# The hand-written step lists of a six-chain graph network kernel laid anew on four engines

## The chip, the cores and the metric

The kernel runs on one core of a Trainium2 chip. The metric is the device time of one execution in microseconds. The kernel before took 2766.72 us (median of 3 runs, 2757.14 to 2768.18).

## The reference, cut to what matters

128 graphs of 128 nodes with 256 features each pass through four residual layers. All graphs share one adjacency matrix, `adj`.

```python
def reference(x, adj, ...):
    h = relu(layernorm(x)); x = x + _L0_gnn_ref(h, adj, ...)   # 4 attention heads, elu, 1 head, elu, 2-layer FFN, layernorm
    h = relu(layernorm(x)); x = x + _L1_gnn_ref(h, adj, ...)   # masked attention with 8 heads of 32, output projection
    h = relu(layernorm(x)); x = x + _L2_gnn_ref(h, adj, ...)   # deg * (h Wi + b) + adj (h Wj)
    h = relu(layernorm(x)); x = x + _L3_gnn_ref(h, adj, ...)   # one attention head; attention output beside its values
    return x
```

## The kernel before, in words

**Tiling.** Two graphs make a pair, so there are 64 pairs. A pair's `x` is a 256 KB tile. It lies in one of 8 slots of the SBUF tensor `xs` (`PAIR_SLOTS = 8`), is loaded there, updated in place by every layer, and stored from there. Pair p+8 uses the slot of pair p.

**Steps.** The work on a pair is cut into steps named by chain: A and B are the heads of the first attention layer, C the rest of layer 0, D and F the eight-head attention of layer 1, E the layers 2 and 3. A suffix .0 or .1 means one graph of the pair. PE has 52 steps for a pair, ACT 56, DVE 83, POOL 17. A step waits on the semaphores of the steps that it reads, or whose buffer it overwrites, does its few instructions and signals. Nothing else orders the engines against each other.

**Order.** Each engine runs its own written list in rounds (`rounds`, L257). An entry `F_rb:6` in round i does step F_rb for pair i-6. The list is walked from front to back in every round, and an engine never goes past a step whose wait has not ended. A larger number thus means a later round, and the place in the list the order inside a round. The rounds of two engines are counted separately: DVE's round i+1 runs about beside PE's round i.

**Load and store.** SyncE (SP) issues both. For each pair it waits for `E_left` (DVE, both graphs) and `E_right` (POOL) of pair p, issues the store (L326), waits until that has landed, and issues the load of pair p+8 (L320). The first step that reads the new tile is `A_stats.0` of pair p+8 on DVE (L810, wait in `x_there`, L801).

**Steps that the text names.**
- `E_o` (PE, L1407), the last matmuls of a pair; `E_left` (DVE, L1026) adds the result into the left half of the slot; `E_right` (POOL, L495) adds the right half.
- `F_recip` (DVE, L978), `F_rb` (DVE, L984: a copy that spreads 16 reciprocals over 512 columns), `F_rT` (PE, L1071: four transposes of that, written to `pF`), then `F_o` (L1329).
- `A_zT` (PE, L1071 into `pA`), the first PE step of a pair; `A_f` (PE, L1080 with `wa`), `A_fround` (ACT, L549), `A_frest` (DVE, L854), `A_wh_hi` and `A_wh_lo` (PE, L1080 with `wh`); `A_wh_lo.0` waits for `A_frest`.
- `F_s` (PE, L1306) and `F_maxa`, `F_maxb` (DVE, L859), `F_suma`, `F_sumb` (DVE, L971), `C_max`, `E_max` (DVE, L859), `B_hl` (DVE, L885), `C_hlow` (DVE, L847), `E_low`, `D_low`, `A_low` (DVE, L839), `E_z`, `D_z`, `A_z` (DVE, L824), `F_x2` (DVE, L998), `B_oh` (PE, L1154), `E_h` (PE, L1384), `E_zT` (PE, L1071 into `pE`), `C_low` (POOL, L465), `D_xb` (POOL, L482), `E_rstd` (POOL, L408 and L410).

In the lists before, the stretch of DVE's list from the end of a pair to the start of the next one in the same slot, and what stands behind it, is:

```python
... E_left.0:8 E_left.1:8 C_hlow:4 F_suma.1:6 F_sumb.1:6 E_low:7 A_stats.0:0 B_hl.1:3 F_recip:6 F_rb:6 A_max.0:2 ...
```

`E_left.1:8` of pair p and `A_stats.0:0` of pair p+8 fall into the same round, p+8. `A_stats.1:0` of the pair comes 20 entries later.

Of the kernel before, what the change touches and what calls it, by code (L numbers as in the profile page):

```python
# [21 lines left out]


PE_ORDER = """
C_hT:3 F_s.1:5 E_pT:7 B_ol.1:2 A_wh_lo.1:1 E_o:7 D_k:4 E_zT:6 F_pTa.1:5 C_hid:3 A_s.0:1 F_pTb.1:5 D_v:4 E_m.0:6 F_rT:5
F_o:5 E_m.1:6 B_oh.1:2 A_wh_hi.1:1 C_ffn:3 E_am:6 A_s.1:1 B_wh0.1:2 D_q:4 A_pT.0:1 B_wh1.1:2 B_wh2.1:2 B_wh3.1:2
F_out:5 A_zT:0 A_pT.1:1 B_ol.0:1 E_zT3:6 C_fT:2 F_s.0:4 C_s:2 A_f:0 E_h:6 B_oh.0:1 A_wh_hi.0:0 C_pT:2 E_fT:6
A_wh_lo.0:0 C_o:2 F_pTa.0:4 B_wh0.0:1 D_zT:3 E_s:6 F_pTb.0:4 B_wh1.0:1 B_wh2.0:1 B_wh3.0:1
""".split()
ACT_ORDER = """  # L30
B_highl.1:4 A_exp.0:3 E_mjhigh.1:8 F_high:7 B_negh.1:4 B_exph.1:4 A_whc_hi.1:3 A_leaky.1:3 B_highh.1:4 A_exp.1:3
A_attn.0:3 B_whc.1:4 D_qc:6 A_high:2 A_attn.1:3 B_negl.0:3 E_hT3:8 C_leaky:4 B_expl.0:3 A_fround:2 C_exp.0:4 E_hc:8
C_exp.1:4 F_expa.0:6 B_negh.0:3 B_exph.0:3 C_attn:4 B_highl.0:3 F_expb.0:6 B_highh.0:3 C_oexp.0:4 C_oexp.1:4 D_high:5
F_pTca.0:6 E_leaky:8 A_whc_hi.0:2 F_pTcb.0:6 A_whc_lo.0:2 E_exp.0:8 E_exp.1:8 B_whc.0:3 C_hhigh:4 E_attn:8 B_negl.1:3
F_expa.1:6 F_expb.1:6 B_expl.1:3 A_whc_lo.1:2 D_kc:5 E_high:7 F_pTca.1:6 F_pTcb.1:6 A_leaky.0:2 C_hidc:4 C_high:4
E_mjhigh.0:7
""".split()
DVE_ORDER = """
E_stats3.1:8 C_moments.1:5 E_moments3.0:8 E_moments3.1:8 C_g.0:5 A_z.0:2 A_z.1:2 E_z3.0:8 A_recip.1:3 E_z3.1:8
A_norm.1:3 C_g.1:5 C_x1.0:5 F_x2:7 A_low:2 C_fTc:4 D_stats.0:5 C_x1.1:5 F_maxa.0:6 C_max.0:4 C_max.1:4 D_moments.0:5  # L40
B_hl.0:3 E_stats.0:7 A_frest:2 D_stats.1:5 D_moments.1:5 F_maxb.0:6 B_hh.0:3 D_z.0:5 B_lowl.0:3 A_moments.0:1
C_recip:4 D_z.1:5 E_fTc:8 E_stats.1:7 F_suma.0:6 F_sumb.0:6 C_min:4 E_moments.0:7 C_h.0:4 E_moments.1:7 C_h.1:4
E_max.0:8 D_low:5 E_max.1:8 E_z.0:7 E_z.1:7 F_maxa.1:6 F_maxb.1:6 E_recip:8 E_left.0:8 E_left.1:8 C_hlow:4 F_suma.1:6
F_sumb.1:6 E_low:7 A_stats.0:0 B_hl.1:3 F_recip:6 F_rb:6 A_max.0:2 E_mi.0:7 E_mjlow.0:7 F_rTc:6 D_vc:5 F_on:6
A_recip.0:2 E_mi.1:7 B_lowl.1:3 A_moments.1:1 E_mjlow.1:7 A_norm.0:2 F_low:6 B_hh.1:3 C_y:4 E_x3:7 A_stats.1:0
C_stats.0:4 C_stats.1:4 A_max.1:2 C_moments.0:4 E_stats3.0:7
""".split()
POOL_ORDER = """
E_fcopy:9 D_rstd:6 B_lowh.0:4 E_right:9 E_rstd:8 A_fleft:3 A_fright:3 C_hb:5 E_xb:8 C_low:5 D_xb:6 C_xb:3 A_rstd:2
B_lowh.1:4 E_rstd3:8 C_rstd:5 C_fcopy:4  # L50
""".split()

STEP_SEMAPHORES = """
# [1419 lines left out]
```

## Time and profile before

| what | value |
|---|---|
| median of 3 runs | 2766.72 us |
| the profiled execution | 2773.31 us |
| its span, first to last instruction | 2771.4 us |
| mean granted TensorE clock | 0.978 of 2.4 GHz |
| PE busy | 2601.7 us (94%) |
| DVE busy | 2228.9 us (80%) |
| ACT busy | 2088.2 us (75%) |
| POOL busy | 1289.6 us (47%) |

The span has three parts. From 0 to 222.6 us the first seven pairs enter and the weights are split; from 222.6 us (`A_zT` of pair 6) to 2571.2 us (`A_zT` of pair 63) all chains run beside each other, 57 rounds; the last 200.2 us are the run-out. An engine's busy time is the time in which it executes; idle time before an instruction is put down to what ended last before it.

### The profile page before, as it was taken

To read this page: it belongs to the slowest core of one execution; us is meant where nothing else is said; L and a number is where in the kernel's file an instruction comes from. 1 tells how busy PE (TensorE), PEld (TensorE's weight loads), DVE (VectorE), ACT (ScalarE), POOL (GpSimd) and SP (SyncE) were. 2 spreads that over 40 slices of the span, in tenths; PEclk is the share of its full clock that TensorE was granted. 3 is DMA by queue.
4 is the path that set the end of the run, shared out by engine and by line. 5 is a ranking of instruction groups with operands and counts; after the bars stand their busy time and mean duration, and the time that the engine had idled before them with its cause. 6 is when DMAs were issued, how large, how long until landed. Compare 5 with 4: busy or idle time off the path is not lost.

```text
span 2771.4 us, 64569 instructions
## 1 busy us (share of the span) xinstructions
PE 2601.7 (94%) x21761; PEld 2349.7 (85%) x21761; DVE 2228.9 (80%) x8352; ACT 2088.2 (75%) x5708; POOL 1289.6 (47%) x2015
## 2 busy tenths in 40 slices
PE   3799999999999999999999999999999999999985
PEld 3788888989889898888988888898988988989873
DVE  4588888878888888888888888887887878888874
ACT  3687787788788787778878777777777778778752
POOL 4444544545454454454544444444444444544431
PEclk9899999999999999999999999999999999999987
DMA  3000000000000000000000000000000000000000
GB/s 126 1 2 9 16 17 9 17 17 9 16 17 13 13 17 14 12 17 17 9 17 17 9 17 17 9 17 17 9 16 17 9 17 17 9 17 13 9 9 12
DMA packets 41288, 44.31 MB, mean 16 GB/s; under 512 B 2817, under 2 KB 40449, under 8 KB 40833
## 3 DMA queue, kind: packets, MB, share of 16 engines
q1 hardware_dynamic: 40816, 39.14, 4.4%
q8 instruction: 176, 2.88, 0.4%
q14 instruction: 152, 1.24, 0.2%
q10 hardware_dynamic: 144, 1.05, 0.1%
HBM read 23.40 MB, written 16.78 MB: 14 GB/s over the span
## 4 chain that ended last, share of the span: by engine, by line
PE 81%; DMA 9%; DVE 6%; issue 2%; ACT 1%; POOL 1%; SPq 0%; DVEq 0%; POOLq 0%; ACTq 0%
PE pA L1080 15%; PE pB L1187 13%; PE pB L1154 8%; PE pB L1080 6%; PE pE L1080 5%; DMA xs<-in_x 4%; PE pC L1080 4%; DMA out_x<-xs 4%; PE pF L1080 3%; PE pF L1316 3%; PE pF L1329 3%; PE pA L1306 3%; PE pE L1384 2%; PE pA L1147 2%; PE pC L1233 2%
## 5 line engine op out<-in xcount | busy, mean ns | idle before, releaser
L459 POOL TENSOR_TENSOR B_h_low<-B_e,B_h_high 128x512 fp32r<-128x512 f32 x128 | 164.9, 1288 | 351.4 <-ACT B_h_high L608 351.4
L672 ACT ACTIVATE F_s_t<-F_s_t,F_m 128x128 f32<-128x128 f32 x1024 | 318.2, 390 | 1.4 <-DVE F_m L859 1.4
L1187 PE MATMUL pB<-wout_high,B_h_high 128*128 128x258 f32 x1024 | 306.5, 299 | 6.3 <-POOL B_h_low L459 6.3
L574 ACT ACTIVATE probs<-probs,A_m 128x128 f32<-128x128 f32 x512 | 199.6, 391 | 128.8 <-DVE A_m L859 128.7
L1187 PE MATMUL pB<-wout_low,B_h_high 128*128 128x258 f32 x1024 | 291.1, 284 | 0.0
L1187 PE MATMUL pB<-wout_high,B_h_low 128*128 128x258 f32 x1024 | 290.9, 284 | 0.0
L1154 PE MATMUL pB<-probs,whs 128*128 128x128 f32 x2048 | 274.0, 277 | 3.1 <-DVE D_v_t L948 1.9
L465 POOL TENSOR_TENSOR C_hid_low<-C_hid_t,C_hid_high 128x512 fp32r<-128x512 f32 x64 | 83.0, 1297 | 416.8 <-ACT C_hid_high L541 416.8
L1154 PEld LDWEIGHTS pB<-probs,whs 128*128 128x128 f32 x2048 | 256.5, 193 | 10.2 <-issue 4.7
L1080 PE MATMUL pA<-wh_high,A_hT_high 128*128 128x512 f32 x512 | 226.4, 442 | 0.7 <-ACT whs L562 0.7
L885 DVE SCALAR_TENSOR_TENSOR B_e<-B_e,pB 128x512 f32<-128x512 f32 x256 | 171.7, 671 | 39.6 <-ACT B_e L600 39.5
L1187 PEld LDWEIGHTS pB<-wout_high,B_h_high 128*128 128x128 f32 x1024 | 194.9, 190 | 9.8 <-POOL B_h_low L459 6.7
L1080 PE MATMUL pA<-wh_low,A_hT_high 128*128 128x512 f32 x512 | 203.1, 397 | 0.0
L1080 PE MATMUL pA<-wh_high,A_hT_low 128*128 128x512 f32 x512 | 202.6, 396 | 0.0
L1187 PEld LDWEIGHTS pB<-wout_low,B_h_high 128*128 128x128 f32 x1024 | 195.6, 191 | 2.9
L1187 PEld LDWEIGHTS pB<-wout_high,B_h_low 128*128 128x128 f32 x1024 | 195.0, 190 | 0.0
L593 ACT ACTIVATE B_e<-pB 128x512 f32<-128x512 f32 x256 | 152.0, 594 | 53.4 <-PE pB L1154 52.3
L681 ACT ACTIVATE F_pT<-pF 128x512 f32<-128x512 f32 x256 | 153.2, 599 | 34.6 <-PE pF L1316 34.5
L608 ACT ACTIVATE B_h_high<-B_e 128x512 fp32r<-128x512 f32 x256 | 159.2, 623 | 17.4 <-DVE B_e L885 17.4
L971 DVE TENSOR_REDUCE F_sum<-F_s_t 128x4 f32<-128x512 f32 x256 | 162.0, 671 | 2.6 <-ACT F_s_t L672 2.6
L600 ACT ACTIVATE B_e<-B_e 128x512 f32<-128x512 f32 x256 | 160.5, 627 | 4.2
L810 DVE BATCH_NORM_STATS2 A_st<-xs 128x6 f32<-128x256 f32 x128 | 54.0, 422 | 130.4 <-DMA xs<-in_x 130.3
(261 smaller groups left out, 9975.3 us busy)
## 6 DMA issues: line engine op xcount, KB each, us to landing
xs<-in_x SPq DMA_DIRECT2D x64, 256.0 KB, 2.7
out_x<-xs SPq DMA_DIRECT2D x64, 256.0 KB, 2.1
probs<-in_a_heads ACTq DMA_DIRECT2D x1, 1024.0 KB, 4.9
F_pT<-in_w_heads SPq DMA_DIRECT2D x2, 512.0 KB, 7.0
xs<-in_w_out SPq DMA_DIRECT2D x1, 1024.0 KB, 9.4
F_s_t<-in_wijT SPq DMA_DIRECT2D x1, 512.0 KB, 6.0
aout_b<-in_a_out SPq DMA_DIRECT2D x1, 256.0 KB, 10.3
D_q_t<-in_w SPq DMA_DIRECT2D x1, 256.0 KB, 6.8
```

Of the source, the lines that this page charges most:

```text
L459: pool.tensor_tensor(B_hl_t[1][:, cols], B_e[:, cols], B_hl_t[0][:, cols].bitcast(F32), ALU.subtract)\
L574: last = act.activation(A_l[:, s, h, :], A_l[:, s, h, :], ACT.Exp, scale=-1.0, bias=A_m[:, s, h:h + 1], accum_out=A_sum[:, s, h:h + 1])
L593: act.activation(B_e[:, cols], pB[:, bank, :], ACT.Relu, scale=-1.0).then_inc(S["B_neg" + part], 1)
L600: act.activation(B_e[:, cols], B_e[:, cols], ACT.Exp, scale=-1.0).then_inc(S["B_exp" + part], 1)
L608: act.activation(B_hl_t[0][:, cols], B_e[:, cols], ACT.Copy).then_inc(S["B_high" + part], 1)
L672: last = act.activation(F_s_t[:, h, :], F_s_t[:, h, :], ACT.Exp, scale=-1.0, bias=F_m[:, s, h:h + 1])
L681: act.activation(F_pT[:, s, c * HPC:(c + 1) * HPC, :].rearrange("p h n -> p (h n)"), pF[:, c, :], ACT.Copy)\
L885: dve.scalar_tensor_tensor(out=e, in0=e, scalar=-1.0, in1=pB[:, bank, :], op0=ALU.add, op1=ALU.max)\
L971: dve.tensor_reduce(total, e, AX.X, ALU.add).then_inc(S["F_sum" + part], 1)
L1080: last = pe.matmul(dst, a, b, start=(i == 0), stop=(i == len(terms) - 1))
L1154: last = pe.matmul(pB[:, bank, (k % 4) * P:(k % 4 + 1) * P], whs[:, s, h, c * P:(c + 1) * P], attnT[:, s, h, :], start=True, stop=True)
L1187: last = pe.matmul(pB[:, 0, 0:D + 2], a, w[:, k, :], start=(k == 0 and i == 0), stop=(k == KH - 1 and i == 2))
```

## The change

Only the four lists change, `PE_ORDER`, `ACT_ORDER`, `DVE_ORDER` and `POOL_ORDER`: the order of their entries and the rounds behind the colons. The steps, their instructions, their waits, the tiles, the slots and SP's program are the same, and so are the steps to which the one-time weight work is tied. The lists before are the removed lines, the new ones the added lines.

```diff
 PE_ORDER = """
-C_hT:3 F_s.1:5 E_pT:7 B_ol.1:2 A_wh_lo.1:1 E_o:7 D_k:4 E_zT:6 F_pTa.1:5 C_hid:3 A_s.0:1 F_pTb.1:5 D_v:4 E_m.0:6 F_rT:5
-F_o:5 E_m.1:6 B_oh.1:2 A_wh_hi.1:1 C_ffn:3 E_am:6 A_s.1:1 B_wh0.1:2 D_q:4 A_pT.0:1 B_wh1.1:2 B_wh2.1:2 B_wh3.1:2
-F_out:5 A_zT:0 A_pT.1:1 B_ol.0:1 E_zT3:6 C_fT:2 F_s.0:4 C_s:2 A_f:0 E_h:6 B_oh.0:1 A_wh_hi.0:0 C_pT:2 E_fT:6
-A_wh_lo.0:0 C_o:2 F_pTa.0:4 B_wh0.0:1 D_zT:3 E_s:6 F_pTb.0:4 B_wh1.0:1 B_wh2.0:1 B_wh3.0:1
+B_wh1.0:2 F_pTb.0:5 D_zT:4 B_wh2.0:2 B_wh3.0:2 E_m.1:6 C_hT:3 F_s.1:5 B_ol.1:2 E_am:6 D_k:4 C_hid:3 A_wh_lo.1:1
+F_pTa.1:5 F_pTb.1:5 D_v:4 F_o:5 A_s.0:1 F_rT:5 E_zT3:6 B_oh.1:2 A_wh_hi.1:1 C_ffn:3 A_s.1:1 E_h:6 B_wh0.1:2 D_q:4
+B_wh1.1:2 E_fT:6 B_wh2.1:2 B_wh3.1:2 A_pT.0:1 E_s:6 F_out:5 A_zT:0 C_fT:2 A_pT.1:1 B_ol.0:1 E_pT:6 F_s.0:4 C_s:2 A_f:0
+E_o:6 B_oh.0:1 A_wh_hi.0:0 A_wh_lo.0:0 E_zT:5 C_pT:2 F_pTa.0:4 B_wh0.0:1 C_o:2 E_m.0:5
...
 DVE_ORDER = """
-E_stats3.1:8 C_moments.1:5 E_moments3.0:8 E_moments3.1:8 C_g.0:5 A_z.0:2 A_z.1:2 E_z3.0:8 A_recip.1:3 E_z3.1:8
-A_norm.1:3 C_g.1:5 C_x1.0:5 F_x2:7 A_low:2 C_fTc:4 D_stats.0:5 C_x1.1:5 F_maxa.0:6 C_max.0:4 C_max.1:4 D_moments.0:5
-B_hl.0:3 E_stats.0:7 A_frest:2 D_stats.1:5 D_moments.1:5 F_maxb.0:6 B_hh.0:3 D_z.0:5 B_lowl.0:3 A_moments.0:1
-C_recip:4 D_z.1:5 E_fTc:8 E_stats.1:7 F_suma.0:6 F_sumb.0:6 C_min:4 E_moments.0:7 C_h.0:4 E_moments.1:7 C_h.1:4
-E_max.0:8 D_low:5 E_max.1:8 E_z.0:7 E_z.1:7 F_maxa.1:6 F_maxb.1:6 E_recip:8 E_left.0:8 E_left.1:8 C_hlow:4 F_suma.1:6
-F_sumb.1:6 E_low:7 A_stats.0:0 B_hl.1:3 F_recip:6 F_rb:6 A_max.0:2 E_mi.0:7 E_mjlow.0:7 F_rTc:6 D_vc:5 F_on:6
-A_recip.0:2 E_mi.1:7 B_lowl.1:3 A_moments.1:1 E_mjlow.1:7 A_norm.0:2 F_low:6 B_hh.1:3 C_y:4 E_x3:7 A_stats.1:0
-C_stats.0:4 C_stats.1:4 A_max.1:2 C_moments.0:4 E_stats3.0:7
+C_max.1:4 A_stats.1:1 F_maxb.0:6 B_lowl.0:3 D_moments.0:5 D_stats.1:5 E_low:7 D_moments.1:5 A_moments.0:1 C_recip:4
+B_hh.0:3 F_suma.0:6 F_sumb.0:6 D_z.0:5 D_z.1:5 C_min:4 E_mjlow.0:7 E_mi.0:7 C_h.0:4 C_h.1:4 A_moments.1:1 D_low:5
+E_mjlow.1:7 E_mi.1:7 F_maxa.1:6 C_hlow:4 F_maxb.1:6 E_x3:7 E_stats3.0:7 F_suma.1:6 F_sumb.1:6 A_stats.0:0
+E_moments3.0:7 E_stats3.1:7 E_moments3.1:7 F_recip:6 F_rb:6 B_hl.1:3 E_z3.0:7 E_z3.1:7 D_vc:5 F_rTc:6 F_on:6 A_max.0:2
+B_lowl.1:3 B_hh.1:3 C_y:4 F_low:6 C_stats.0:4 A_max.1:2 C_stats.1:4 A_recip.0:2 C_moments.0:4 C_moments.1:4 A_norm.0:2
+E_fTc:7 C_g.0:4 A_z.0:1 A_recip.1:2 C_g.1:4 A_z.1:1 C_x1.0:4 A_norm.1:2 E_max.0:7 E_max.1:7 C_x1.1:4 F_x2:6 C_fTc:3
+E_recip:7 E_stats.0:6 A_low:1 E_stats.1:6 E_moments.0:6 D_stats.0:4 E_moments.1:6 F_maxa.0:5 E_z.0:6 C_max.0:3
+B_hl.0:2 E_left.0:7 A_frest:1 E_z.1:6 E_left.1:7
 """.split()
 POOL_ORDER = """
-E_fcopy:9 D_rstd:6 B_lowh.0:4 E_right:9 E_rstd:8 A_fleft:3 A_fright:3 C_hb:5 E_xb:8 C_low:5 D_xb:6 C_xb:3 A_rstd:2
-B_lowh.1:4 E_rstd3:8 C_rstd:5 C_fcopy:4
+D_xb:6 E_rstd:7 E_xb:7 D_rstd:5 B_lowh.0:3 A_fleft:2 A_fright:2 C_xb:4 E_rstd3:7 C_low:4 C_hb:4 B_lowh.1:3 E_fcopy:7
+A_rstd:1 C_rstd:4 C_fcopy:3 E_right:7
 """.split()
```

ACT's 56 entries are laid anew in the same way.

## Rows read from the trace of the kernel before

**Rows 1.** Busy time by stretch: start, 57 full rounds, run-out (PE, PEld, DVE, ACT, POOL, PEclk, DMA).

```profile
0.00:222.58 222.58, 162.28 (x1148) 144.66 (x1148) 141.25 (x501) 134.97 (x345) 100.35 (x138) 0.94 0.12 40
222.58:2571.17 2348.59, 2282.66 (x19383) 2071.76 (x19381) 1954.29 (x7353) 1847.33 (x5073) 1128.98 (x1769) 0.99 0.05 14
2571.17:2771.40 200.23, 156.78 (x1236) 133.31 (x1234) 133.37 (x501) 105.94 (x290) 60.24 (x110) 0.85 0.03 10
```

**Rows 2.** Waits in the full rounds, 222.58 to 2571.17: us in total, times, longest.

```profile
DVE A_st L810 <- DMA xs<-in_x: 125.4, 56, 3.9
...
PE pF L1071 <- DVE F_rb_t L984: 65.2, 32, 2.6
```

**Rows 3.** The chain that ended last, 1061 to 1071 us: start, us, what.

```profile
1061.03 4.03 DMA out_x<-xs
...
1065.08 2.68 DMA xs<-in_x
...
1070.16 0.90 PE pF L1071 x3
```

**Rows 4.** DVE in order of time, 1060 to 1071 us (idle before in brackets).

```profile
1060.39 0.61 DVE L1026 SCALAR_TENSOR_TENSOR xs<-pE,E_rec,xs 128x128 f32<-128x128 f32 x2 [1.22 <-PE pE L1407]
1060.92 0.68 DVE L847 TENSOR_TENSOR C_hT_low<-pC,C_hT_high 128x512 fp32r<-128x512 f32 x1
1061.52 1.27 DVE L971 TENSOR_REDUCE F_sum<-F_s_t 128x4 f32<-128x512 f32 x2
...
1067.85 0.43 DVE L810 BATCH_NORM_STATS2 A_st<-xs 128x6 f32<-128x256 f32 x1 [3.43 <-DMA xs<-in_x]
...
1069.06 1.04 DVE L984 COPY F_rb_t<-F_rec 128x512 f32<-128x512 f32 x1
```

**Rows 5.** DMA issues: out<-in, queue, count, KB, median us to landing.

```profile
xs<-in_x SPq DMA_DIRECT2D x64, 256.0 KB, 2.7
out_x<-xs SPq DMA_DIRECT2D x64, 256.0 KB, 2.1
```

**Rows 6.** Busy time by stretch, three single rounds (`A_zT` to `A_zT`).

```profile
1041.43:1085.31 43.88, 41.27 (x342) 37.21 (x341) 34.63 (x131) 32.53 (x89) 19.83 (x32) 0.96 0.05 14
...
1126.46:1166.31 39.85, 39.81 (x343) 36.16 (x342) 33.92 (x131) 32.34 (x89) 19.77 (x32) 1.00 0.04 14
2531.60:2571.17 39.57, 39.57 (x343) 36.25 (x341) 33.68 (x129) 32.30 (x89) 19.95 (x33) 1.00 0.03 8
```

**Rows 7.** PE in order of time, 1416 to 1421 us: `A_f`, `E_h`, `B_oh.0`, `C_pT`.

```profile
1416.26 0.36 PE L1080 MATMUL pA<-A_hT_high,wa_high 128*128 128x256 f32 x1
...
1417.05 1.05 PE L1384 MATMUL pE<-w_w,E_h3T 128*128 128x130 f32 x8
1417.94 1.05 PE L1154 MATMUL pB<-probs,whs 128*128 128x128 f32 x8
...
1420.22 0.38 PE L1209 MATMUL pC<-ident,C_l 128*128 128x128 f32 x2
```

**Rows 8.** DVE in order of time, 1416 to 1419 us: `F_maxa.0`, `C_max.0`, `A_frest`.

```profile
1416.36 0.27 DVE L859 CUSTOM_DVE_ANT_0 F_s_t<-pA,mask 128x128 f32<-128x128 f32 x1
...
1417.20 0.27 DVE L859 CUSTOM_DVE_ANT_0 C_l<-pC,mask 128x128 f32<-128x128 f32 x1
...
1418.73 0.43 DVE L854 TENSOR_TENSOR A_f_t<-pA,A_f_t 64x256 fp32r<-64x256 f32 x1
```

**Rows 9.** Line 824 over the whole span: ns min/median/max.

```profile
L824 DVE TENSOR_SCALAR E_z_t<-xs,E_mv,E_rs x256: 383/415/1081, 198.2 to 2757.0; 128x256 f32<-128x256 f32 x128
```

**Rows 10.** Tile `F_rb_t` over the whole span: ns min/median/max.

```profile
L984 DVE COPY F_rb_t<-F_rec x64: 426/428/1527, 170.3 to 2721.5; 128x512 f32<-128x512 f32 x64
```

**Rows 11.** POOL in order of time beside the `F_rb` of rows 4.

```profile
1068.55 1.27 POOL L482 TENSOR_TENSOR xs<-xs,bo_b 128x512 f32<-128x512 f32 x1
```

**Rows 12.** DVE in order of time, the last two `E_left` of the run-out.

```profile
2742.61 0.61 DVE L1026 SCALAR_TENSOR_TENSOR xs<-pE,E_rec,xs 128x128 f32<-128x128 f32 x2 [2.28 <-PE pE L1407]
...
2768.26 0.61 DVE L1026 SCALAR_TENSOR_TENSOR xs<-pE,E_rec,xs 128x128 f32<-128x128 f32 x2 [2.28 <-PE pE L1407]
```

More of the change, by code:

```diff
@@ L29 @@
+F_pTa.1:5 F_pTb.1:5 D_v:4 F_o:5 A_s.0:1 F_rT:5 E_zT3:6 B_oh.1:2 A_wh_hi.1:1 C_ffn:3 A_s.1:1 E_h:6 B_wh0.1:2 D_q:4
+B_wh1.1:2 E_fT:6 B_wh2.1:2 B_wh3.1:2 A_pT.0:1 E_s:6 F_out:5 A_zT:0 C_fT:2 A_pT.1:1 B_ol.0:1 E_pT:6 F_s.0:4 C_s:2 A_f:0
+E_o:6 B_oh.0:1 A_wh_hi.0:0 A_wh_lo.0:0 E_zT:5 C_pT:2 F_pTa.0:4 B_wh0.0:1 C_o:2 E_m.0:5
 """.split()
 ACT_ORDER = """
-B_highl.1:4 A_exp.0:3 E_mjhigh.1:8 F_high:7 B_negh.1:4 B_exph.1:4 A_whc_hi.1:3 A_leaky.1:3 B_highh.1:4 A_exp.1:3
-A_attn.0:3 B_whc.1:4 D_qc:6 A_high:2 A_attn.1:3 B_negl.0:3 E_hT3:8 C_leaky:4 B_expl.0:3 A_fround:2 C_exp.0:4 E_hc:8
@@ L33 @@
[L33 to L36, printed above, removed]
+B_negl.1:2 F_expb.1:5 D_kc:4 B_expl.1:2 F_pTca.1:5 F_pTcb.1:5 C_hidc:3 A_whc_lo.1:1 A_leaky.0:1 C_high:3 B_highl.1:2
+E_hT3:6 B_negh.1:2 B_exph.1:2 A_whc_hi.1:1 B_highh.1:2 F_high:5 A_leaky.1:1 E_hc:6 A_exp.0:1 A_exp.1:1 D_qc:4
@@ L37 @@
+B_whc.1:2 E_leaky:6 A_attn.0:1 E_exp.0:6 E_exp.1:6 A_high:0 A_attn.1:1 E_attn:6 B_negl.0:1 C_leaky:2 B_expl.0:1
+A_fround:0 F_expa.0:4 C_exp.0:2 B_highl.0:1 B_negh.0:1 C_exp.1:2 B_exph.0:1 E_high:5 C_attn:2 A_whc_hi.0:0 F_expb.0:4
+B_highh.0:1 C_oexp.0:2 C_oexp.1:2 E_mjhigh.0:5 F_pTcb.0:4 F_pTca.0:4 D_high:3 B_whc.0:1 E_mjhigh.1:5 A_whc_lo.0:0
+C_hhigh:2 F_expa.1:4
 """.split()
 DVE_ORDER = """
-E_stats3.1:8 C_moments.1:5 E_moments3.0:8 E_moments3.1:8 C_g.0:5 A_z.0:2 A_z.1:2 E_z3.0:8 A_recip.1:3 E_z3.1:8
```

## The prediction

> **What bounds the kernel now.** I read the busy time by stretch first, then the waits, the chain, and DVE in order of time.
>
> In the 57 full rounds the span is 2348.6 us, or 41.20 us a round, and PE is busy 2282.7 us of it; no other engine is over 84% busy [rows 1]. So PE is the engine to watch, and it is idle for 65.9 us. The waits name one cause for nearly all of it: PE waits for `F_rb`, 65.2 us in 32 waits. DVE itself waits 125.4 us in 56 rounds of 57 for the load of `xs` [rows 2].
>
> The chain shows that these two are one. `E_left` of a pair ends at 1061.0; the store runs 4.03 us; the load of the next pair of the slot 2.68 us; `A_stats.0` starts at 1067.85, `F_rb` at 1069.06, and PE gets `F_rT` at 1070.16 [rows 3, 4]. DVE's list has between `E_left.1` and `A_stats.0` only `C_hlow`, two sums and `E_low`: 0.6 + 1.3 + 0.6 = about 2.5 us [rows 4], against 4.8 us for a median store and load (2.1 + 2.7) [rows 5] and 6.7 in this round. DVE stands for the rest, and `B_hl.1`, `F_recip` and `F_rb` stand behind it. A tile that is not needed for a long time thus holds up a copy that is needed at once.
>
> **What a round costs without it.** Three single rounds tell [rows 6]. The worst takes 43.88 us: 2.61 us of PE idle, and a mean clock of 0.96 where the others have 1.00, so part of the stretch ran at 1.2 instead of 2.4 GHz. PE busy there is 41.27 against 39.81, so the clock costs some 1.5 us more. A round in which the load came in time takes 39.85. In the last full round no load is awaited any more, and it takes 39.57 with PE busy for all of it. PE's work is the same under any order, so 39.57 is the floor, and 41.20 - 39.57 = 1.63 us a round, 93 us in all, is what stands to be won here.
>
> **The change, part by part.**
>
> (1) The load's room. In the new lists `E_left.1:7` is the last entry of DVE's list and `A_stats.0:0` the 32nd. Pair p ends its slot at the end of round p+7, and pair p+8 starts in round p+8, after 31 entries. Among these are three `F_max` halves of 0.84 us each (four scores, 1416.36 to 1417.20 [rows 8]), four sums of 0.63 and six operations on 512 columns of 0.6 (`B_lowl`, `B_hh`, `E_low`, `D_low`, `C_hlow`, `E_x3`, priced as `C_hlow`) [rows 4]: 2.5 + 2.5 + 3.6 = 8.6 us, without 18 smaller ones. Store and load take 6.7 us in rows 3, and about 7.2 where DVE's wait is the longest, 3.9 instead of 3.4 [rows 2, 4]. So the wait goes in every round. SP's own place does not matter: it issues two DMAs a round. The store also waits for `E_right`, the last of POOL's list; that list is some 20 us of work in a round of 40 [rows 6], and `C_fcopy:3` and `C_rstd:4` ahead of it read results from the middle of DVE's list, so it comes before `E_left.1`. Even if it came 1.4 us after it, the load would be in time.
>
> (2) `F_rb`. It now stands five places behind `A_stats.0`, which has nothing to wait for, and `F_rT` stands one step later on PE, behind `F_o` and `A_s.0`. Nothing of the old chain is left between them. Gain: all of the 65.9 us and the clock's share.
>
> (3) Steps past each other. 52, 56, 83 and 17 entries get new neighbours. PE's sum does not change: the same products in another order. I allow 0.1 us either way. What can change is where an engine waits. The tightest place that I find: `A_wh_lo.0` on PE waits for `A_frest` on DVE, and ahead of `A_frest` DVE now has `F_maxa.0`, `E_z.0`, `C_max.0`, `B_hl.0` and `E_left.0`. DVE needs 0.84 + 0.42 + 0.21 + 0.6 + 0.3 + 0.43 = 2.8 us from the start of `F_maxa.0` [rows 4, 8, 9], and that start is 0.10 us after `A_f`'s [rows 7, 8]. PE has from the start of `A_f`: `A_f` 0.79, `E_o` about 0.45 (half of the 0.89 of `E_h`, which has twice its products), `B_oh.0` and `A_wh_hi.0` 2.28 [rows 7], 3.5 us. So 0.6 us are spare there. If that is used up, PE waits, and behind it stand `A_wh_lo.0` and `E_zT` of the next pair. Over the whole list I bound the cost of such places from 0 (as in the last round of rows 6) to 0.7 us a round (the price of rival 1), and take 0.13, nearest to the clean rounds of before, which are 39.57 and 39.85. A round then takes 39.70.
>
> (4) Depth. On PE the way from `A_zT` to `E_o` of a pair was 7 rounds less 24 of 52 places, 6.54 rounds, and is now 6 rounds and 8 places, 6.15. The run-out of 200.2 us has PE idle for 43 us and a clock of 0.85 [rows 1]; its last pairs follow each other at 25.65 us [rows 12], an E chain alone. 0.39 of such a round is 10 us; the gain may be 0 if that chain sets the end anyway. I take 5. For the start, with its weight work and 60 us of idle PE, I take nothing, within 5 us either way.
>
> **Sum.** 57 x (41.20 - 39.70) = 85.5, and 5: 90.5 us. The profiled execution took 2773.3 us (span 2771.4), so 2682.8. It lies 6.6 us above the median of the runs shown, whose spread is 11 us; since stores of 2 or 4 us would no longer move the end, I expect less of that afterwards and take off 3: **2680 us**, 3.1% less. 0.5% (14 us) is about what a measurement of this kernel can tell from no change.
>
> **The rivals.**
>
> *Rival 1: about half is given back to the SBUF port.* `F_rb` takes 0.43 us mostly but up to 1.53 [rows 10]. In the chain's round it started 0.51 us into POOL's `D_xb` (1068.55, 1.27 us) and ended 0.28 us after it [rows 4, 11]: it stood until POOL was through. `E_z` too goes from 0.42 to 1.08 [rows 9]. The new lists place such copies and normalisations against other POOL steps. If in each round one that PE waits for is held for one POOL instruction, 1.27 us, where 0.6 us are spare, PE loses 0.67 us a round, 38 us: 2718 us. Against it: at `E_z.0` POOL has done `E_rstd` and waits for `E_z.1`, so it is quiet just where room is short.
> The Trainium skill, "SBUF — State Buffer", section "SBUF: two separate sides", says of the port pair that VectorE and GpSimd share that whichever starts first has it for its whole instruction and the other fully blocks. By this rule a mere reordering of unchanged work can cost time, which speaks against this change; the trace agrees, with the 1.04 us of this `F_rb`.
>
> *Rival 2: no change.* The load wait goes, and another wait of the same size stands behind it, in PE's list order or because PE's own time per round is 41 and not 39.7. Against it: 39.57 and 39.85 with the same matmuls. It would give 2755 to 2780.
>
> *Rival 3: slower.* The place is `A_frest` before `A_wh_lo.0`: DVE's six entries ahead of it now tie `F_s`, `E_rstd`, `C_s` and `E_o` together, and if one comes late, all do. To cost more than it wins, `A_frest` must be late by the spare 0.6 and the gain of 1.5 and 0.24 (14 us over 57 rounds) each time: from 2.3 us on. If PE then stands 2.6 us in each round, as it did at worst for `F_rb`, with full clock, a round is 39.7 + 2.6 = 42.3: 57 x 1.1 = 63 us more, less 5, about 2825 us. Nothing in the sums comes near 2.3 us.
>
> **How the numbers follow.** Forecast 0.74; rival 1, with other partial losses between 2700 and 2752, 0.15; rival 2 0.06; rival 3 0.05. Faster by over 0.5%: 0.89; within: 0.06; slower: 0.05. The forecast's own bounds: floor rounds of 39.57 (93 us) with the full 10 us of depth, 5 of the start and 6.6 of the median give 2652; rounds of 39.85 with nothing at the ends give 2696. Rival 1 reaches to 2718. The range is 2655 to 2718.
>
> **What would show it.** Right: DVE's wait at L810 for `in_x` is gone or below 5 us in all; PE's wait for `F_rb` too; full rounds of 39.6 to 39.9 us with a clock of 1.00; the chain nearly all PE, with no DMA in it after the start. Rival 1 shows as PE waits on L824, L984 or L914 steps whose mean length has grown. Wrong: PE idle of over 1 us a round under any name, above all at L1080 into `pA` behind `A_frest`, or PE busy per pair above 40 us.

## The result, and the profile after

The changed kernel takes 2730.41 us (median of 4 runs, 2727.86 to 2731.97) against 2761.93 us before (4 runs, 2753.94 to 2768.18). The ratio is 0.9887, 95% interval 0.9855 to 0.9918: 1.1% faster, where 3.1% was forecast, and 12 us above the range. The runs lie closer together than before, 4 us apart instead of 14. The traces compared below are of an execution of 2773.31 us before and of 2727.86 us after, which is 45 us apart where the medians are 31.5 us apart.

The first two parts of the page of the changed kernel, and its chain by engine:

```profile
span 2725.9 us, 64569 instructions
...
PE 2604.2 (96%) x21761; PEld 2345.3 (86%) x21761; DVE 2310.8 (85%) x8352; ACT 2057.9 (75%) x5708; POOL 1322.8 (49%) x2015
...
PE 56%; DVE 19%; ACT 14%; POOL 5%; issue 5%; DMA 0%; SPq 0%; DVEq 0%; POOLq 0%; ACTq 0%
```

The transfers are off the chain. But DVE does the same instructions as before and is now busy for 2310.8 us instead of 2228.9, and only 56% of the chain is PE's. Busy time by stretch (columns as in [rows 1]: PE, PEld, DVE, ACT, POOL, clock, DMA), for the 57 full rounds, the run-out and one single round:

```profile
224.06:2530.28 2306.22, 2284.07 (x19382) 2070.47 (x19381) 2037.69 (x7355) 1816.94 (x5074) 1157.33 (x1767) 1.00 0.05 14
2530.28:2725.90 195.62, 153.00 (x1219) 128.15 (x1217) 136.10 (x496) 105.33 (x287) 64.71 (x108) 0.89 0.03 11
1397.39:1437.85 40.46, 40.08 (x342) 36.33 (x341) 35.75 (x132) 31.86 (x90) 20.33 (x31) 1.00 0.05 14
```

2306.22 / 57 = 40.46 us a round, against 41.20 [rows 1] and the 39.70 of the forecast. The rounds hardly vary any more: 55 of the 57 take 40.5 us, two 40.2. So the pattern of [rows 6] is gone, with its dips of the clock, and something that is the same in every round has come in. The run-out is 195.6 instead of 200.2 us; the first seven pairs take 224.1 instead of 222.6. Together: 42.4 + 4.6 - 1.5 = 45.5 us, the difference of the two spans (2771.4 and 2725.9).

PE's waits in the full rounds (us in total, times, longest) name two steps:

```profile
PE pC L1196 <- POOL C_f L433: 12.3, 55, 0.2
...
PE pB L1071 <- DVE D_z_t L824: 9.8, 57, 0.2
```

`F_rb` [rows 2] is not among them any more, and DVE has no wait for `in_x`. The two are `C_fT` and `D_zT`, 0.2 us each time. A wait this short stands for more, because the end of the matmul before it overlaps it. Start to start, `A_zT` to `C_fT` takes 0.82 us, and 0.53 where nothing is late (third experiment); `F_pTb.0` to `D_zT` takes 0.77, and 0.44.

Behind both stands one thing. DVE and POOL of the changed kernel in order of time; DVE first:

```profile
1409.71 1.66 DVE L824 TENSOR_SCALAR D_z_t<-xs,D_mv,D_rs 128x256 f32<-128x256 f32 x2
...
1428.24 1.60 DVE L893 TENSOR_TENSOR B_h_low<-B_e,B_h_high 128x512 fp32r<-128x512 f32 x1
1429.77 0.68 DVE L885 SCALAR_TENSOR_TENSOR B_e<-B_e,pB 128x512 f32<-128x512 f32 x1
```

```profile
1409.60 1.29 POOL L459 TENSOR_TENSOR B_h_low<-B_e,B_h_high 128x512 fp32r<-128x512 f32 x1 [0.65 <-ACT B_h_high L608]
...
1428.00 1.29 POOL L477 TENSOR_TENSOR C_e<-C_h_t,b_b 128x512 f32<-128x512 f32 x1
```

The line at 1409.71 is `D_z.0` and `D_z.1` together. `D_z.0` starts 0.11 us after POOL's `B_lowh.0` and takes 1.34 us instead of 0.41. `B_lowl.1` starts 0.24 us after POOL's `C_hb` and takes 1.61 instead of 0.68. `D_z.0` ends 0.15 us and `B_lowl.1` 0.55 us after POOL's instruction has, each less than it takes when alone. In all 57 full rounds these lengths are the same within 0.01 us. In return `F_rb` is down from 0.79 to 0.43 us on average and `E_z.1` from 0.64 to 0.41; those holds of before are gone. The way from the second hold to PE, from the chain:

```profile
1428.32 1.03 DVE B_h_low L893
...
1429.77 0.69 DVE B_e L885
...
1433.72 1.74 ACT probs L574 x9
1435.45 0.72 ACT D_q_t L663 x2
1436.17 0.28 ACT wh L615
...
1436.52 1.02 POOL C_f L427
...
1438.67 0.22 PE pC L1196
```

`B_lowl.1` holds `B_hh.1` behind it on DVE; ACT's `B_highh.1` waits for that, and with it all that stands behind it in ACT's list, `F_high`, `A_leaky.1`, `E_hc`, both `A_exp`, `D_qc`, up to `B_whc.1`; then POOL's `C_fcopy`, then `C_fT` on PE. Six entries of ACT's list stand between, and none of them reads what `B_lowl.1` writes. How much of the delay is left at the end of this way shows in the fifth experiment.

### The profile page after: what moved, and what is told of

The parts are those of the page before. It is cut to its first block, busy times and chain, and to the rows that moved or that the text cites. A ratio compares the mean times of both kernels' runs of the same rounds, so it can differ in the third digit from the quotient of the medians.

```text
span 2725.9 us, 64569 instructions
## 1 busy us (share of the span) xinstructions
PE 2604.2 (96%) x21761; PEld 2345.3 (86%) x21761; DVE 2310.8 (85%) x8352; ACT 2057.9 (75%) x5708; POOL 1322.8 (49%) x2015
## 3 DMA queue, kind: packets, MB, share of 16 engines
q10 hardware_dynamic: 144, 1.05, 0.1%
## 4 chain that ended last, share of the span: by engine, by line
PE 56%; DVE 19%; ACT 14%; POOL 5%; issue 5%; DMA 0%; SPq 0%; DVEq 0%; POOLq 0%; ACTq 0%
PE pA L1080 12%; PE pB L1154 7%; PE pB L1080 7%; ACT probs L574 6%; PE pB L1187 4%; PE pE L1080 4%; PE pC L1080 4%; DVE D_z_t L824 3%; DVE B_e L885 3%; DVE F_sum L971 3%; PE pA L1306 3%; PE pF L1329 2%; DVE B_h_low L893 2%; POOL C_f L427 2%; PE pF L1316 2%
## 5 line engine op out<-in xcount | busy, mean ns | idle before, releaser
L672 ACT ACTIVATE F_s_t<-F_s_t,F_m 128x128 f32<-128x128 f32 x1024 | 326.2, 396 | 54.2 <-DVE F_m L859 54.2
L1187 PE MATMUL pB<-wout_high,B_h_high 128*128 128x258 f32 x1024 | 312.4, 305 | 0.9 <-POOL B_h_low L459 0.8
L1154 PE MATMUL pB<-probs,whs 128*128 128x128 f32 x2048 | 280.8, 281 | 2.0 <-DVE D_v_t L948 0.6
L408 POOL TENSOR_TENSOR E_ve<-E_mv,eps 128x2 f32<-128x2 f32 x128 | 25.0, 195 | 482.0 <-DVE E_mv L817 481.9
L681 ACT ACTIVATE F_pT<-pF 128x512 f32<-128x512 f32 x256 | 139.2, 595 | 107.1 <-PE pF L1316 107.0
L1080 PE MATMUL pA<-wh_high,A_hT_high 128*128 128x512 f32 x512 | 214.5, 419 | 0.7 <-ACT whs L562 0.7
L488 POOL TENSOR_TENSOR xs<-xs,bl_b 128x512 f32<-128x512 f32 x64 | 83.2, 1300 | 162.6 <-DVE E_z_t L824 162.6
```

What stands on the lines that cost most here:

```text
L488: pool.tensor_tensor(pair_slot(p), pair_slot(p), on_pair(bl2_b[:, :]), ALU.add).then_inc(S["E_xb"], 1)
L672: last = act.activation(F_s_t[:, h, :], F_s_t[:, h, :], ACT.Exp, scale=-1.0, bias=F_m[:, s, h:h + 1])
L681: act.activation(F_pT[:, s, c * HPC:(c + 1) * HPC, :].rearrange("p h n -> p (h n)"), pF[:, c, :], ACT.Copy)\
L1080: last = pe.matmul(dst, a, b, start=(i == 0), stop=(i == len(terms) - 1))
L1154: last = pe.matmul(pB[:, bank, (k % 4) * P:(k % 4 + 1) * P], whs[:, s, h, c * P:(c + 1) * P], attnT[:, s, h, :], start=True, stop=True)
L1187: last = pe.matmul(pB[:, 0, 0:D + 2], a, w[:, k, :], start=(k == 0 and i == 0), stop=(k == KH - 1 and i == 2))
```

## The experiments

The ratios are to runs of the kernel before that were made beside each set: median 2767.43 us for experiments 1 to 4, 2765.63 us for 5 to 7. The changed kernel was not run again beside them, so a difference to its 2730.41 us carries the few us by which these medians differ from 2761.93; the rounds of the traces are the sharper measure.

**1 and 2. One entry of each collision moved.** In POOL's list `C_hb` goes to where POOL is idle; in DVE's, `D_z` goes ahead of two sums.

```diff
-... C_xb:4 E_rstd3:7 C_low:4 C_hb:4 B_lowh.1:3 ...
+... C_xb:4 C_hb:4 E_rstd3:7 C_low:4 B_lowh.1:3 ...
```

> The changed kernel with one entry of POOL's list moved: C_hb stands right behind C_xb, where POOL is idle for 6.5 us, instead of behind C_low, where it ran beside B_lowl.1 on DVE (1.61 us there, 0.68 before). Theory port (DVE's operation is held until POOL's ends, and both stalls lie on one loop of 40.47 us): B_lowl.1 back to 0.7 us, the loop 0.9 us shorter, rounds fall from 40.47 to PE's own 39.6, so about 50 us less than the changed kernel's 2730: 2680. Theory order (the loop through A_max, A_exp and C_fcopy is too long even without stalls): B_lowl.1 short, but rounds stay at 40.3 or more, 2715 to 2730.

```diff
-... B_hh.0:3 F_suma.0:6 F_sumb.0:6 D_z.0:5 D_z.1:5 C_min:4 ...
+... B_hh.0:3 D_z.0:5 D_z.1:5 F_suma.0:6 F_sumb.0:6 C_min:4 ...
```

> The changed kernel with one move in DVE's list: D_z.0 and D_z.1 ahead of F_suma.0 and F_sumb.0, so that D_z.0 no longer meets B_lowh.0 on POOL (1.34 us there, 0.41 before). Theory port: D_z.0 back to 0.4 us and D_zT on PE no longer waits; the same loop loses 0.9 us and two more sums of 1.2 us ahead of D_z, so rounds of 39.6 to 39.8, 2680 to 2695. Theory order: rounds stay above 40.3, 2715 to 2730.

Measured: the first 2714.72 us (0.9805 of before, interval 0.9768 to 0.9841), the second 2709.46 (0.9789, 0.9759 to 0.9819). Full rounds of 40.17 and 40.10 us. `B_lowl.1` took 0.69 in the first, `D_z.0` 0.41 in the second, and the other one was held as before in each. Neither theory's number came: the rounds fall by 0.29 and 0.36 us, which is neither all of the excess nor nothing. The second move does two things at once: it ends the hold and it starts `D_z` two sums, some 1.2 us, earlier. But in the trace of the changed kernel `D_z.1` ends at 1411.37, 0.05 us before `D_zT` starts. PE could take `D_zT` 0.33 us sooner (0.77 less 0.44), and without the hold `D_z.1` would end 0.93 us sooner. By these numbers the end of the hold alone is enough, with 0.6 us to spare; no run tried it without the earlier place.

**3. Both moves.**

> Both moves. Theory port: as either alone, since PE's own 39.6 a round is then the floor and the second move has nothing left to win: 2675 to 2685. If each stall cost its own 0.45 us a round (two loops), e1 and e2 would each give about 2705 and only this one 2680. Theory order: 2710 or more.

Measured: 2689.13 us (0.9718, 0.9688 to 0.9747), 57 rounds of 39.79. The two gains add: 40.46 - 0.29 - 0.36 = 39.81. So they are not two parts of one loop beside PE, as I had thought, but two separate places at which PE is late. At `D_zT` the price is the 0.93 us of hold less the 0.6 us that the lists leave spare; at `C_fT` it comes about in another way (fifth experiment). Busy time by stretch for the full rounds:

```profile
221.34:2489.56 2268.22, 2268.22 (x19383) 2071.79 (x19381) 1943.77 (x7353) 1828.79 (x5074) 1122.25 (x1768) 1.00 0.05 15
```

PE is busy for the whole of it, and no wait of PE is listed. So 39.79 us is what PE itself takes in the new order, 0.18 us more than in the old one (fourth experiment). DVE's busy time is down by 94 us from the changed kernel's 2037.69.

**4. The load's room alone, in the kernel before.** One entry moves.

```diff
-... E_low:7 A_stats.0:0 B_hl.1:3 F_recip:6 F_rb:6 ... E_x3:7 A_stats.1:0 ...
+... E_low:7 B_hl.1:3 F_recip:6 F_rb:6 ... E_x3:7 A_stats.0:0 A_stats.1:0 ...
```

> The kernel before with one entry moved: A_stats.0:0 stands 19 places later on DVE, just ahead of A_stats.1:0, behind F_rb. It tests the load's room alone. My theory (the load wait delays F_rb and cost 41.20 - 39.8 us a round): DVE's wait for in_x gone, PE's wait for F_rb gone, rounds of 39.6 to 39.8, 2763 - 85 = about 2680. Rival (something else in the old lists also holds the round at 41): 2740 or more.

Measured: 2683.34 us (2682.15 to 2685.60; 0.9698, 0.9668 to 0.9728), 57 rounds of 39.6. Full rounds and run-out by stretch, and the chain by engine:

```profile
222.08:2479.85 2257.77, 2257.77 (x19383) 2063.86 (x19382) 1936.89 (x7353) 1834.41 (x5073) 1125.19 (x1769) 1.00 0.05 15
2479.85:2682.60 202.75, 158.91 (x1236) 135.06 (x1234) 132.95 (x501) 106.09 (x290) 60.19 (x110) 0.84 0.03 10
```

```profile
PE 94%; DVE 2%; ACT 2%; POOL 1%; issue 1%; DMA 0%; SPq 0%; DVEq 0%; ACTq 0%; POOLq 0%
```

2257.77 / 57 = 39.61. Neither PE nor DVE waits for what they waited for in [rows 2]. This is the fastest kernel of the study, 47 us below the changed one, with one entry moved out of 208: the room for the load is worth all that the forecast gave it, and the rest of the new order takes more than half of that back.

**5. Half of the POOL instruction, all lists as changed.** `C_hb` adds `b2` for the first graph of the pair only; for the second, the elu's value is left without its sum and `b2`.

```diff
-pool.tensor_tensor(C_hb_t[:, :, :], C_h_t[:, :, :], on_pair(b2_b[:, :]), ALU.add)
+pool.tensor_tensor(C_hb_t[:, 0, :], C_h_t[:, 0, :], b2_b[:, :], ALU.add)
```

> The changed kernel with all lists as they are, but C_hb on POOL does one graph of the pair only (256 columns instead of 512, about 0.65 us instead of 1.29), so the second graph's sum lacks b2 and the ffn's residual. Theory port with slack: B_lowl.1 on DVE is still held, but by 0.3 us instead of 0.9, which is under the 0.6 us that are spare on the way to C_fT; rounds fall by the same 0.30 us as in e1, to 40.17, 2715 us. Rival, proportional: each 0.1 us of the hold costs its third on PE, rounds of 40.26, 2720. Rival, no port: the hold stays at 0.9 us and rounds at 40.47.

Measured: 2712.86 us (0.9801, 0.9764 to 0.9839), rounds of 40.17, as the theory of port and slack had it. DVE's step and POOL's, in order of time:

```profile
1420.99 1.05 DVE L893 TENSOR_TENSOR B_h_low<-B_e,B_h_high 128x512 fp32r<-128x512 f32 x1
```

```profile
1420.76 0.74 POOL L477 TENSOR_TENSOR C_e<-C_h_t,b_b 128x256 f32<-128x256 f32 x1
```

POOL's instruction is 0.55 us shorter, and DVE's is too (1.05 against 1.60), with no list touched and DVE's own work the same. That settles what holds it. The remaining hold, 0.36 us, costs nothing: the rounds are those of the first experiment, where there is none. So the price has a threshold, not a slope.

Where the threshold comes from stands in the traces of the first and of this experiment. It is not the fixed 0.6 us that I had expected. ACT's `B_whc.1` and POOL's `C_fcopy` behind it in the first experiment, then `B_whc.1` in this one:

```profile
1428.05 0.39 ACT L615 ACTIVATE wh<-pB 128x258 f32<-128x258 f32 x1 [0.46 <-PE pB L1187]
...
1428.52 0.68 POOL L427 TENSOR_TENSOR C_f<-wh,zeros 128x4 bf16<-128x4 f32 x1 [1.13 <-ACT wh L615]
```

```profile
1428.67 0.39 ACT L615 ACTIVATE wh<-pB 128x258 f32<-128x258 f32 x1 [0.30 <-PE pB L1187]
```

In both `B_whc.1` waits for PE, 0.46 and 0.30 us, and `C_fcopy` starts 1.48 us before `A_zT` in every round: the delay of `B_lowl.1` has been used up by then. In the changed kernel ACT comes without a wait, and `C_fcopy` starts 1.33 us before `A_zT`. Of 0.92 us of hold thus only 0.14 us arrive there. But `C_fcopy` itself then takes 2.10 us instead of 1.56, and ends 0.67 us later in all. Of these, 0.39 us are spare ahead of `C_fT`, and PE pays the other 0.29.

**6. The wait kept, but behind `F_rb`.** In the kernel before:

```diff
-... E_low:7 A_stats.0:0 B_hl.1:3 F_recip:6 F_rb:6 A_max.0:2 ...
+... E_low:7 B_hl.1:3 F_recip:6 F_rb:6 A_stats.0:0 A_max.0:2 ...
```

> The kernel before with A_stats.0:0 only three places later on DVE, right behind F_rb. The load is still awaited there: 4.8 to 7.2 us from E_left's end against 2.5 + 0.9 us of DVE work and idle, 1.3 us of the three entries; so DVE should still wait for in_x some 0.3 to 2.5 us a round. Theory (what counts is who stands behind the wait): PE no longer waits for F_rb, and A_max.0 and E_mi.0, now behind the wait, have about a microsecond of room: rounds of 39.6 to 39.9, 2683 to 2695. Rival (DVE's idle time itself is what the round loses): rounds of 40.3 and more, 2715 or more.

Measured: 2693.93 us (0.9736, 0.9698 to 0.9773), rounds of 39.76, both within what the theory gave. Waits in the full rounds:

```profile
DVE A_st L810 <- DMA xs<-in_x: 46.2, 51, 2.6
...
PE pE L1080 <- DVE E_mj_low L1004: 11.0, 13, 1.2
```

DVE still waits for the load in 51 rounds, and PE loses 11 us where it had lost 65. Moving the same wait past three entries won 72 us; taking it away altogether won another 11. (The wait is also shorter, 46.2 us in all instead of 125.4, so length and place are not fully parted; but over a third of the wait is left, and a sixth of PE's loss.)

**7. The room taken back, in the changed kernel.**

```diff
-... A_moments.0:1 C_recip:4 ... F_sumb.1:6 A_stats.0:0 E_moments3.0:7 ...
+... A_moments.0:1 A_stats.0:0 C_recip:4 ... F_sumb.1:6 E_moments3.0:7 ...
```

> The changed kernel with the load's room taken back: A_stats.0:0 stands right behind A_moments.0:1, about 3 us of DVE work behind E_left.1, instead of 13.5. Theory: DVE waits for in_x again, 2 to 4 us in each round, and what stands behind it (B_hh.0, F_suma.0, D_z) goes to PE late: rounds of 42 us or more, 2800 to 2880, slower than before. Rival (the new lists are robust, the room was not the point): 2730 to 2745.

Measured: 2858.35 us (1.0323, 1.0274 to 1.0373), 42.66 us a round, again within what the theory gave. Waits in the full rounds:

```profile
PE pB L1071 <- DVE D_z_t L824: 109.4, 57, 3.4
DVE A_st L810 <- DMA xs<-in_x: 90.9, 56, 3.1
...
PE pC L1196 <- POOL C_f L433: 13.2, 55, 0.2
```

With the old distance of some 3 us between `E_left.1` and `A_stats.0`, the new lists are slower than the old ones: the load wait now delays `D_z` and so `D_zT`, where the lists leave little spare. The delay also tests the hold on `D_z.0`: in 56 of the rounds it starts 0.36 us into `B_lowh.0` instead of 0.11, takes 1.05 us instead of 1.34, and ends 0.15 us after it as before. The change gains nothing without that one distance.

## Why the prediction was wrong

**Bound and part (1), right.** The load's wait goes, the clock's dips with it, and rounds without it take what [rows 6] showed: 39.61 us in the fourth experiment, 57 times, against the 39.57 and 39.85 read. The time forecast for the change, 2680, is within 4 us of what this one move gives. That is in part luck: the fourth experiment has none of the 5 us of part (4), and its rounds are 0.09 us (5 us in all) below the forecast's 39.70. One bound is added up wrongly, without effect on the result: from 2773.3, the floor 93 + 10 + 5 + 6.6 us lower is 2659, not 2652, which starts from the median and takes the 6.6 off twice.

**Part (2), right.** PE does not wait for `F_rb` any more.

**Part (3), the step that failed.** "and take 0.13", the price of steps that now wait for each other, on top of a floor of 39.57 that was held to be "the same under any order": a round was to take 39.70 us and takes 40.46. Three terms make up the excess of 0.85 us over 39.61 us:

| term | us a round | how it is known |
|---|---|---|
| `C_fT` late, behind `B_lowl.1` held by `C_hb` and the longer `C_fcopy` that comes with it | 0.29 | 0.82 to 0.53 start to start; rounds 40.46 to 40.17 in experiments 1 and 5 |
| `D_zT` late, behind `D_z.0` held by `B_lowh.0` | 0.36 | 0.77 to 0.44 start to start; rounds 40.46 to 40.10 in experiment 2 |
| PE's own neighbours | 0.18 | PE busy without a wait, 39.79 in experiment 3 against 39.61 in experiment 4 |

They sum to 0.83 of the 0.85. Against the 39.70 of the forecast a round is 0.76 us too long, 43 us in all; the rest of the 50 us between forecast and median is the 3 us taken off at the end, 1.5 us of the start and 2.6 us by which the median lies above the execution in the trace. Within this part three things were wrong. I looked for the tightest place by eye and settled on `A_frest` before `A_wh_lo.0`; it does not appear among PE's waits. I priced DVE's steps there at lengths from the trace of before, which hold only while POOL is quiet beside them. And I allowed 0.1 us either way for PE's new neighbours, put it at nothing in the sum, and 0.18 came. That this third term is there is measured; where it comes from is read, not tested: a few single-matmul or row-split steps (`E_fT`, `F_o`, `F_rT` behind `A_s.0`) now follow others and start some 0.1 us later after them. No run moved these alone.

**Part (4), right in size.** The run-out is 4.6 us shorter (5 forecast); the start 1.5 us longer (nothing, within 5). That the depth is the reason was not tested. In the traces of the kernels with the old lists the run-out takes 200.2 to 202.8 us, and in those with the new ones 195.6 to 199.2.

**The rivals.** Rival 1 is what happened, and it had 0.15. Its mechanism was right, a DVE step held for one POOL instruction with 0.6 us spare (at `D_zT` 0.93 of hold costs 0.36), and so was its sign, a PE wait on an L824 step whose length has grown. Its place was not, and it priced one such place at 0.67 us a round. There are two, of 0.29 and 0.36; that their sum is almost the same 38 us is luck. That they would sit exactly where the new lists need DVE could have been asked of the diff: POOL's neighbours in time of every two-input or normalising step on DVE that stands before a PE step. The argument against it, that POOL is quiet at `E_z.0`, is true and answers for one step of many; `E_z.1` did get shorter. Rival 2 is out by the fourth experiment. Rival 3 did not come, though the seventh experiment shows how near it lay.

The rule of the Trainium skill that I had weighed, in "SBUF — State Buffer", section "SBUF: two separate sides", says that of a VectorE and a GpSimd instruction on their shared port pair one blocks the other for its whole length. The trace agrees, and experiment 5 puts it to the test: 0.55 us less on POOL are 0.55 us less on DVE. What a hold costs the kernel is another matter: 0.93 us were held each time, and what PE paid was what the spare time did not cover.

## What to carry to other kernels

In lists walked in order, the price of a wait is set by who stands behind it, so look for the urgent step behind the patient one, and move that one entry first: it may give all there is. Before relaying everything, lay POOL's long instructions beside DVE's copies, normalisations and two-input steps that an idle-free engine needs: a list whose durations come from a quiet trace has holds of up to one POOL instruction that it does not know of. And ask what each hold costs after the spare time: at `B_lowl.1` a hold of 0.36 us was free and one of 0.92 cost 0.29, most of it by pushing a later step into a second collision.

## What the runs showed that I had not expected

The hold works in both directions. `C_fcopy`'s first instruction on POOL writes 4 elements a partition and takes 0.20 us when alone, as the same step of chain E does, but 1.01 us in nearly every round of the changed kernel. POOL, and DVE beside it:

```profile
1436.52 1.01 POOL L427 TENSOR_TENSOR C_f<-wh,zeros 128x4 bf16<-128x4 f32 x1 [0.60 <-ACT wh L615]
```

```profile
1436.39 0.47 DVE L941 SCALAR_TENSOR_TENSOR xs<-C_y_t,C_rs,xs 128x256 f32<-128x256 f32 x1
1436.79 0.67 DVE L877 TENSOR_TENSOR probs<-probs,A_rec 128x512 f32<-128x512 f32 x1
```

It starts inside DVE's `C_x1.0` and ends 0.07 us after DVE's `A_norm.1`, two steps with two tensor inputs in SBUF each. That they hold it is read from these rows; no run moved them alone. In the first, third and fifth experiments `C_fcopy` starts 0.14 us earlier against PE and takes 1.56 us as a whole instead of 2.10. These 0.54 us are the larger part of the 0.67 us by which it is late in the changed kernel: with 0.39 us spare, the 0.14 us that are left of the hold on `B_lowl.1` would have cost PE nothing by themselves. But the hold is what brings the second collision about: without it DVE's `A_norm.1` is 0.48 us earlier against PE, and `C_x1.0` has just ended when `C_fcopy` starts.

The kernel before also showed idle times of PE of 2.6, 1.4 or no us and hardly any between. After the change PE's waits are of 0.2 us, and with the transfers off the path 55 of 57 rounds take the same time within 0.1 us.
